# Pair 3's query product moved behind pair 1's scores and two turned scores, step 0 reordered, constant rows made later

## What is computed

```python
x = x + xattn(layernorm(x), ctx, ctx, Wq, bq, Wk, bk, Wv, bv, Wo, bo)
#   q, k, v = projections;  scores = q @ k.T / 4;  attn = softmax(scores)
#   heads = attn @ v;  concat @ Wo + bo
x = x + ffn(layernorm(x), router_w, w1, w2)
#   probs = softmax(logits);  top 2 of 8;  out += w * (gelu(x @ w1.T) @ w2.T)
```

## Time and profile before

| | us |
|---|---|
| median of 3 runs | 450.44 |
| lowest and highest | 448.28 and 453.13 |
| the profiled execution, its own time | 451.83 |
| span of the profiled execution | 450.0 |
| what lies around the span | 1.8 |
| the stretch that the change touches (end of the prologue and step 0) | 33.5 to 54.7 of the span |

### The profile page before, as it was taken

How to read it: one execution, slowest core, us unless ns; L and a number is a source line. 1 busy time by engine, 2 the same in 40 slices (tenths; PEclk the granted TensorE clock), 3 DMA queues, 4 the chain that set the end, 5 groups by cost and what they waited for, 6 DMA issues and landing times.

```text
span 450.0 us, 8730 instructions
## 1 busy us (share of the span) xinstructions
PE 399.1 (89%) x2762; PEld 333.1 (74%) x2763; DVE 276.1 (61%) x644; ACT 237.2 (53%) x440; POOL 201.6 (45%) x185
## 2 busy tenths in 40 slices
PE   7777898999999998758899999999999899999940
PEld 3555674867767765526899999999999899999930
DVE  2887866647467657786966556644468865744310
ACT  1896555556445563333656457444567745644410
POOL 4957667361551222114245455354433664543320
PEclk9998998999998999759999999999999999999985
DMA  8414553362510112655545533532227722232220
GB/s 243 132 39 90 121 123 103 68 153 53 136 54 0 54 49 65 218 187 162 214 118 150 134 70 100 159 61 49 47 40 230 220 47 47 38 55 25 23 30 12
DMA packets 25303, 44.09 MB, mean 98 GB/s; under 512 B 6416, under 2 KB 19856, under 8 KB 22608
## 3 DMA queue, kind: packets, MB, share of 16 engines
q0 software_dynamic: 8320, 14.99, 18.2%
q1 hardware_dynamic: 13440, 25.79, 18.0%
q10 hardware_dynamic: 3504, 2.83, 2.0%
HBM read 30.73 MB, written 12.86 MB: 97 GB/s over the span
## 4 chain that ended last, share of the span: by engine, by line
PE 68%; DVE 9%; DMA 5%; ACT 5%; issue 4%; POOL 2%; POOLq 0%; ACTq 0%; DVEq 0%
PE ps_s L1850 20%; PE ps_t L1867 14%; PE ps_t L1870 7%; DMA result<-big,rowtok 4%; PE ps_s L1497 3%; PE ps_t L1547 2%; DVE mx L1018 2%; PE ps_a L1572 2%; PE ps_a L1570 2%; PE ps_t L1544 2%; PE ps_c L1572 2%; PE ps_c L1832 2%; DMA big<-rows,gtok 2%; PE ps_c L1570 2%; PE ps_c L1457 2%
## 5 line engine op out<-in xcount | busy, mean ns | idle before, releaser
L621 POOL DMA_INDIRECT result<-big,rowtok x38 | 63.9, 1682 | 112.5 <-DMA result<-big,rowtok 62.8
L1850 PE MATMUL ps_s<-xgT,KB 128*128 128x256 f32 x912 | 110.9, 280 | 3.0 <-DVE xgT L1368 3.0
L1850 PEld LDWEIGHTS ps_s<-xgT,KB 128*128 128x128 f32 x912 | 108.6, 188 | 4.2 <-DVE xgT L1368 1.7
L1018 DVE TENSOR_REDUCE mx<-ps_s 128x4 f32<-128x616 f32 x64 | 49.2, 797 | 32.5 <-PE ps_s L1497 32.3
L589 POOL DMA_INDIRECT big<-rows,gtok x38 | 44.8, 1178 | 32.7 <-DVE gtok L1325 14.9
L686 ACT ACTIVATE big<-ps_t 128x512 f32<-128x512 f32 x80 | 45.3, 593 | 22.3 <-PE ps_t L1547 19.0
L1867 PE MATMUL ps_t<-KB,HTb 128*128 x160 | 56.9, 397 | 0.0
L902 ACT ACTIVATE big<-ps_t,wrow 128x256 f32<-128x256 f32 x38 | 18.1, 477 | 65.7 <-PE ps_t L1870 63.2
L1867 PE MATMUL ps_t<-KB 128*128 x144 | 51.9, 403 | 0.0
L1384 DVE TENSOR_TENSOR HTb<-big,HTb 128x512 fp32r<-128x512 f32 x40 | 27.6, 692 | 31.6 <-ACT big L894 31.6
L894 ACT ACTIVATE big<-ps_s 128x512 f32<-128x512 f32 x76 | 45.4, 597 | 0.0
(11 more groups left out here) (240 smaller groups left out, 712.4 us busy)
## 6 DMA issues: line engine op xcount, KB each, us to landing
VP<-in_wexp SPq DMA_DIRECT2D x8, 1024.0 KB, 5.3
big<-in_wexp SPq DMA_DIRECT2D x8, 1024.0 KB, 5.0
qd<-big SPq DMA_DIRECT2D x24, 128.0 KB, 2.3
KB<-qd POOLq DMA_DIRECT2D x6, 512.0 KB, 5.4
result<-x SPq DMA_DIRECT2D x8, 256.0 KB, 3.1
rows<-xn SPq DMA_DIRECT2D x8, 256.0 KB, 2.9
KB<-qd POOLq DMA_DIRECT2D x6, 256.0 KB, 6.1
XS<-in_x ACTq DMA_DIRECT2D x1, 1024.0 KB, 5.2
```

Source lines behind the costliest of these rows:

```text
L621: pool.indirect_dma_start(out, bass.IndirectOffsetOnAxis(rowtok[:, u, h:h + 1], 0), ys[:, 2 * (u % 2) + h, :], None, compute_op=ALU.add).t ...
L1018: dve.tensor_reduce(mx[:, i, :, 2 * k:2 * k + 2].rearrange("p a b -> p b a"), ps_s[n % 2][:, :, 0:2 * KEYS].rearrange("p b (h k) -> p b h ...
L1850: last = mm(ps_s[j // 4][:, j // 2 % 2, (j % 2) * PAIR:(j % 2 + 1) * PAIR], w1[:, w, k, j * P:(j + 1) * P], xgT[:, u % 2, a, k, :], start= ...
```

## The change

On PE, the first half and the second half of `q_product(3)` stood between scores of pair 1; now the product stands in one piece behind all eight scores of pair 1 and behind `turned_scores(0, 0)` and `turned_scores(0, 1)`, which stood behind `maxima_transposes(1)` before. `xn_transposes(3)` moves from behind `scores(1, 3)` to behind `scores(1, 6)`. Step 0 gets an order of its own, in which scores of pair 2 and turned scores of pair 0 alternate from `scores(2, 1)` on. On ACT, `exp(0, 0)` and `exp(0, 1)` stand ahead of `evac_q(3)` and `evac_maxima(1)`; `evac_xnT(4)` moves behind `exp(0, 4)` and `evac_q(4)` behind `exp(0, 6)`; the two constant-row instructions of sequence 1 move to step 0 (behind `exp(0, 5)`) and to step 1 (behind `exp(1, 0)`). On DVE, `statistics1(4)` moves from behind the fourth to behind the sixth maximum of pair 1.

```diff
 # ACT, prologue and step 0
             evac_xnT(3)
-            ones(1)
-            evac_q(3)
-            evac_maxima(1)
+            def first_step():
+                for n in range(2):
+                    exp(0, n)
+                evac_q(3)
+                evac_maxima(1)
+                for n in range(2, 5):
+                    exp(0, n)
+                evac_xnT(4)
+                exp(0, 5)
+                ones(1, (0,))
+                exp(0, 6)
+                evac_q(4)
+                for n in range(7, 10):
+                    exp(0, n)
+                evac_maxima(2)
 # ACT, step(m)
+                if m == 0:
+                    first_step()
+                    return
                 if has(0):
                     exp(m, 0)
+                if m == 1:
+                    ones(1, (1,))
 # DVE
-            for n in range(4):
+            for n in range(6):
                 maxima(1, n)
             dve.wait_ge(ld_x2, 16)
             statistics1(4)
-            for n in range(4, 8):
+            for n in range(6, 8):
                 maxima(1, n)
             negatives(1)
 # PE, prologue
-            for n in range(4):
+            for n in range(7):
                 scores(1, n)
             xn_transposes(3)
-            for n in range(4, 6):
-                scores(1, n)
-            q_product(3, (0,))
-            for n in range(6, 8):
-                scores(1, n)
-            q_product(3, (1,))
+            scores(1, 7)
+            turned_scores(0, 0)
+            turned_scores(0, 1)
+            q_product(3)
             maxima_transposes(1)
 # PE, step 0
+            def first_step():
+
+                scores(2, 0)
+                for n in range(1, 5):
+                    scores(2, n)
+                    if n < 4:
+                        turned_scores(0, n + 1)
+                xn_transposes(4)
+                turned_scores(0, 5)
+                scores(2, 5)
+                turned_scores(0, 6)
+                q_product(4)
+                scores(2, 6)
+                turned_scores(0, 7)
+                scores(2, 7)
+                for n in range(8, 10):
+                    turned_scores(0, n)
+                maxima_transposes(2)
 # PE, step(m)
                 if m == 0:
-                    turned_scores(0, 0)
-                    turned_scores(0, 1)
+                    first_step()
+                    return
```

More of the change, by code:

```diff
@@ L1762, in step @@
                     value_sums(m - 1, 1)
-                if has(0) and m:
+                if has(0):
                     turned_scores(m, 0)
@@ L1776, in step @@
                 if has(0):
-                    if m:
-                        turned_scores(m, 1)
+                    turned_scores(m, 1)
                     turned_scores(m, 2)
```

## The result

| | before | after |
|---|---|---|
| median, us (20 runs each) | 451.61 | 455.91 |
| lowest to highest | 448.16 to 455.94 | 452.02 to 458.37 |
| span of the profiled execution | 450.0 | 454.7 |
| mean granted clock of the profiled execution | 0.953 | 0.943 |

The changed kernel takes 1.0086 of the time of the kernel before, 95% interval [1.0063, 1.0108]: 3.9 us slower. The 3.9 us are worked out from the ratio; the medians of the table are 4.3 apart. The forecast was 3.9 us slower than before. All ratios are of the fast runs of both kernels, those up to 1.5% above the fastest, while the column on half rate further down has every run (with fast runs alone the kernel before would have 41.5 there and not 42.4).

A forecast was written before the change was run, and what follows sets the result against it. PE was taken to bound the kernel, busy 89% of the span and 68% of the chain. Late queries 2.4 plus half rate in step 1 1.5 gave 3.9 us slower, 454.3 us; range 449.8 to 457.0.

The forecast's parts named there:

- The direction and the total: Whole kernel: 3.9 us slower, 454.3 us beside the median of 450.44.
- The wait for `md`: End of prologue: PE waits 1.5 us, from 37.8 to 39.3, ahead of `turned_scores(0, 0)`, with `q_product(3)` queued behind.
- the rival with a landing of 5.5: Read of `md` ahead of `turned_scores(0, 0)` lands in 5.5 us, not 3.5: 2.0 us more, +5.9, 456.3; chance 0.12.
- The late queries: Prologue to step 1: `evac_q(3)` 2.7 us late at half rate; through a 13.3 us serial chain `scores(3, 0)` 2.4 late.
- The cause of the first half-rate stretch: End of prologue: the half rate moves from 36.0 to about 39.4, behind the `md` wait, onto the product.
- Step 0 is shorter, for nothing: Step 0: last transposes through at 52.2 or 53.6, `residual` collision gone; PE then waits 3.1 or 3.5 us for pair 3's queries.
- The half rate in step 1: Step 1: idle time ahead of `scores(3, 0)` brings half rate, costing 1.5 us more; bounds 0 and 1.7.
- The small edits: Later `ones`, later `statistics1(4)` and POOL's delayed norm and reads: all hidden, taken as 0.
- The two that were to refute it: Wrong if PE's idle stretch ahead of the first turned matmul is missing, or step 2's first scores (72.77 before) come no later.
- Three others: Signs: about 1.5 us idle ahead of the first turned matmul; step 0's last transposes before 54; over 2 us idle ahead of step 1.

The follow-up runs named there:

- e2: Kernel before with only the changed prologue (product behind the turned scores, `statistics1(4)` later, two exponentials ahead of `evac_q(3)`), step 0 as before: 453.65 against 451.68, 1.0040.
- changed again: The changed kernel as it is, run once more for a second profile: 454.75 against 451.25 for the kernel before, 1.0080.
- e5: Changed kernel with 9 matmuls on constants in PE's second new wait only, behind step 0's last maxima transposes: 453.03 against 452.18 for the kernel before, 1.0030.
- e6: Changed kernel without the wait for the read of `md`: pair 0's maxima replaced by zeros read early. 454.17 against 452.18 for the kernel before, 1.0043.
- e1: Changed kernel with `q_product(3)` put ahead of the two turned scores and `evac_q(3)` ahead of their exponentials: 453.19 against 451.68 for the kernel before, 1.0037.
- e9: e2 with `q_product(3)` ahead of the two turned scores and `evac_q(3)` ahead of their exponentials: 451.36 against 451.25 for the kernel before, 1.0011.
- e3: Kernel before with only the changed step 0 (alternating scores and turned scores) and later constant rows, prologue as before: 451.67, 0.9997 of the kernel before.
- e4: Changed kernel with matmuls on constants in both new PE waits, 5 ahead of `turned_scores(0, 0)`, 9 behind step 0's last maxima transposes: 453.84 against 451.68 before, 1.0042.
- e7: e1 with matmuls on constants between pair 1's scores and 6 behind step 0's last maxima transposes: 453.28 against 452.18 for the kernel before, 1.0038.

## Why the prediction was right

**The direction and the total.** Right: 3.9 us forecast, 3.9 measured. That the two agree to a tenth is luck, since the terms were less exact than the sum. In the profiles they are 2.1 at `scores(3, 0)` (2.4 forecast), 3.0 in step 1 (1.5 forecast) and 1.5 back in step 2 (nothing forecast). The time itself, 454.3 forecast and 455.91 measured, is off by more, as three runs had put the kernel before at 450.44 where twenty put it at 451.61.

**The wait for `md`.** Right in kind, but mis-sized: 1.5 us forecast, 0.76, 0.67 and 0.36 us measured (changed, e2, changed again), and 1.32 in e5. PE came to it 0.9 later than forecast, because `scores(1, 6)`, the transposes and `scores(1, 7)` already ran at half rate. This mattered little, since what releases PE is the landing: forecast 7.35 us behind `maxima_transposes(0)`, measured 7.47. Landing took about 3.2 us from the issue at 37.86 to the matmul at 41.08, against the rival with a landing of 5.5. By the fit of the Trainium skill ("DMA: Bandwidth & Descriptors", Anatomy of one DMA) for a DMA from GpSimd an estimate would be 2.1 us; the trace doesn't agree. e6 shows what the wait is worth at `evac_q(3)`: 0.8.

**The late queries.** `evac_q(3)` was forecast 2.7 late at half rate and is 2.8 and 2.2 late; `scores(3, 0)` forecast 2.4 late, measured 2.1 and 1.8. The chain in between is as long as it was, 13.0 us instead of 13.3. From the first turned matmul to `evac_q(3)` it took 4.40 us, 4.4 forecast. By e1 and e9 it is the place of the product that does it.

**The cause of the first half-rate stretch.** This step was wrong. I put it behind the wait for `md`, by moving the stretch of the kernel before from 36.0 to 39.4. It did not move: it begins at 37.8, 4.2 us behind `maxima_transposes(0)` as before (4.1) and 3.3 us ahead of the first turned matmul, and it stands in e6 and e9, which don't have that wait. It lasts 6.8 us and not 3.4. The number came out right by luck, because most of the product lies in it either way. Why it lasts twice as long stays open.

**Step 0 is shorter, for nothing.** Right in kind, but too large: from `scores(2, 0)` to the last maxima transposes it takes 10.8 us, 11.6 before and 9.8 forecast. These transposes start 22.56 behind those of pair 0, 22.60 before, although `scores(2, 0)` came 0.8 us later (11.80 against 10.97). e3 shows the same from the other side: no gain. One detail was wrong: the collision with POOL's `residual` didn't vanish but moved, as DVE's first operation of `negatives(2)` now lasts 1.45 us (0.18 for pair 1's) across it. DVE's timeline:

```profile
54.45 1.45 DVE L1047 TENSOR_SCALAR nm<-mx 128x32 fp32r<-128x32 f32 x1
```

and POOL's:

```profile
54.56 1.28 POOL L492 TENSOR_TENSOR XS<-XS,bo_sb 128x512 f32<-128x512 f32 x1
```

That is most of why the wait for `qd` is 1.88 and not the forecast 3.5: DVE holds PE for 1.27 just ahead of it. The end of the wait is unchanged, so it costs nothing.

**The half rate in step 1.** Right that it would come, wrong in size: 1.5 us forecast, 3.0 measured in the profile, as the stretch is twice as long. It begins at 58.2, in the wait for `qd`, and e4 and e5 speak for idle time there as its cause; e3, which has the stretch without that wait, shows that others can bring it too. The second half of it was made up by step 2's stretch, which is missing after; nothing in the forecast said that. Over all runs the time at half rate is 4.5 to 6.7 us longer than before. If PE were on the path in all of it, that would be 2.2 to 3.3 of the 3.9 us (half of the time at half rate, from 42.4, 46.9 and 49.1); this division is an estimate.

**The small edits.** Right: `ones` fits in, and POOL's later norm and reads of pairs 4 and 5 release nobody late; e3, which has the later constant rows, takes the same time as before.

**The signs.** The two that were to refute it did not appear: PE idles ahead of the first turned matmul, and step 2's first scores come later (79.48, which is 77.8 by the clock of the profile before, against 72.77). `evac_q(3)`, at 43.8 by that clock, lies in its 42 to 44. Three others came short: that idle time is 0.76 and not about 1.5, the last transposes of step 0 start at 54.5 by that clock and not before 54, and the wait ahead of step 1 is 1.88 and not over 2.

## What to carry to other kernels

When a product feeds a long serial chain (here store, wait, load: 13 us from `evac_q` to the first scores, with 0.3 us of slack), put nothing ahead of it that can wait for a DMA, however well it fills idle slots. Work that is made ready earlier gains nothing while the next instruction in the same queue waits for something that has become later. And idle time of PE can cost more than itself if the clock falls with it: compare kernels by the mean clock of many runs, since the place of the half-rate stretches in one profile is partly chance.

## What the runs showed of the hardware that I had not expected

- PE stayed at half rate for 6.8 us while it was busy without a gap (6.60 of 6.60 us in e6). Being busy again didn't restore full rate at once here, and the stretches were of about 3.4, 6.8 and 10.2 us, with one of 17 where the attention part ends. What decides the length stays open.
- Filling one gap with matmuls moved the half-rate stretch to other work instead of removing it (e7 from the product to step 0). Both versions with fillings between pair 1's scores came out 0.4% slower than the kernel before.
- Single executions of one kernel differ by 6 to 8 us (448.16 to 455.94, 452.02 to 458.37), more than the whole effect; POOL waited for the four stores of `qd` for 3.9 us in most profiles, and for 5.05 (e6) and 5.28 (e5) in two.
